# The turned row maxima of the second attention: copied by ScalarE and added by GpSimd instead of added by VectorE

## The reference, cut to what matters

```python
q = (x @ Wq.T).reshape(b, s, H, HD)
k = (x @ Wk.T).reshape(b, s, H, HD)
v = (x @ Wv.T).reshape(b, s, H, HD)
f = jax.nn.log_sigmoid((x @ Wf.T + bf).astype(jnp.float32))
c = jnp.cumsum(f, axis=1)
scores = jnp.einsum('bihd,bjhd->bhij', q, k) * scale
scores = scores + (c[:, :, None, :] - c[:, None, :, :]).transpose(0, 3, 1, 2)
scores = jnp.where(causal[None, None], scores, -jnp.inf)
p = jax.nn.softmax(scores, axis=-1)
o = jnp.einsum('bhij,bjhd->bihd', p, v).reshape(b, s, D)
return o @ Wo.T
```

## Time and profile before

| What | Value |
|---|---|
| Median of three runs | 1497.99 us (1496.64 to 1499.35) |
| The profiled execution | 1496.76 us, its span 1494.9 us |
| Loop of the second attention | from about 838 to 1287 us of the span |
| Its steady unit | 14.04 us (a unit's group 0 starts at 1010.10 and the next one's at 1024.14 us) |
| VectorE, whole span | busy 1147.7 us (77%) |
| TensorE, whole span | busy 1111.0 us (74%) |
| ScalarE, GpSimd, whole span | busy 909.8 us (61%), 469.7 us (31%) |

### The profile page before, as it was taken

How to read it: one execution, slowest core, us unless ns; L and a number is a source line. 1 busy time by engine, 2 the same in 40 slices (tenths; PEclk the granted TensorE clock), 3 DMA queues, 4 the chain that set the end, 5 groups by cost and what they waited for, 6 DMA issues and landing times. The chain is left out here.

```text
span 1494.9 us, 26800 instructions
## 1 busy us (share of the span) xinstructions
PE 1111.0 (74%) x7861; PEld 520.7 (35%) x7861; DVE 1147.7 (77%) x3607; ACT 909.8 (61%) x1823; POOL 469.7 (31%) x676
## 2 busy tenths in 40 slices
PE   1556666666532899994476889999999999677995
PEld 1112222222222566662253432332333333243554
DVE  4699999999979444444856699999999999377664
ACT  1699999999851344332552466666666666356453
POOL 0133233323215677774100122222222222123331
PEclk9755555555555899997697899999999999798998
DMA  2366777777717222224534111111111111400001
GB/s 56 105 121 136 144 144 133 142 139 138 128 41 201 63 77 79 78 78 145 172 107 138 63 57 59 57 57 57 58 58 58 57 57 37 113 1 1 1 14 43
DMA packets 220767, 127.66 MB, mean 85 GB/s; under 512 B 164353, under 2 KB 200321, under 8 KB 220369
## 3 DMA queue, kind: packets, MB, share of 16 engines
q1 hardware_dynamic: 200576, 100.10, 27.4%
q0 software_dynamic: 6320, 15.54, 3.2%
q10 hardware_dynamic: 13728, 10.30, 2.8%
HBM read 54.33 MB, written 37.62 MB: 62 GB/s over the span
## 5 line engine op out<-in xcount | busy, mean ns | idle before, releaser
L1849 ACT ACTIVATE qkv_made<-qkv_lower 128x1024 f32<-128x1024 f32 (+3 forms) x256 | 208.0, 872 | 94.0 <-PE qkv_lower L1666 94.0
L521 PE MATMUL a_sc<-a_k,a_q 16*128 16x512 bf16 (+3 forms) x384 | 165.4, 504 | 123.9 <-DVE a_mx L700 117.3
L2012 DVE CUSTOM_DVE_ANT_0 all_y<-qkv_upper,all_mask 128x384 bf16<-128x384 f32 (+3 forms) x512 | 231.5, 485 | 17.3 <-PE qkv_upper L1630 11.2
L1630 PE MATMUL qkv_upper<-l_k,all_y 64*128 64x512 bf16 (+3 forms) x768 | 208.7, 334 | 48.3 <-DVE qkv_mx L2016 25.6
L1895 POOL TENSOR_SCALAR_AFFINE_SELECT qkv_made<-qkv_made 128x256 f32<-128x256 f32 x256 | 102.5, 406 | 408.7 <-ACT qkv_made L1849 318.7
L700 DVE CUSTOM_DVE_ANT_0 a_rows<-a_sc,all_mask 128x1024 bf16<-128x1024 f32 (+7 forms) x256 | 192.3, 751 | 7.9 <-PE a_sc L521 7.4
L570 ACT ACTIVATE a_rows<-a_rows 128x1024 bf16<-128x1024 bf16 (+7 forms) x256 | 171.3, 669 | 24.3 <-DVE a_rows L710 24.3
L2016 DVE TENSOR_REDUCE qkv_mx<-qkv_upper 128x1 f32<-128x512 f32 x256 | 173.0, 686 | 7.5 <-PE qkv_upper L1630 7.3
L1666 PE MATMUL qkv_lower<-all_y,l_k 64*128 64x384 bf16 (+3 forms) x768 | 173.4, 330 | 7.0 <-DVE all_y L2033 1.2
L1685 PE MATMUL qkv_upper<-qkv_made,qkv_v_heads 128*32 128x384 f32 (+3 forms) x1920 | 177.8, 434 | 0.0
L579 ACT ACTIVATE a_unread<-a_rows 128x1024 bf16<-128x1024 bf16 (+7 forms) x256 | 170.9, 668 | 0.0
(11 more groups left out here) (255 smaller groups left out, 1968.4 us busy)
## 6 DMA issues: line engine op xcount, KB each, us to landing
qkv_made<-out_rows SPq DMA_DIRECT2D x16, 512.0 KB, 8.1
l_k<-k_rows SPq DMA_DIRECT2D x64, 128.0 KB
o_rows<-qkv_made SPq DMA_DIRECT2D x32, 256.0 KB, 2.0
all_y<-q_rows SPq DMA_DIRECT2D x128, 48.0 KB
a_raw<-in_gate ACTq DMA_DIRECT2D x16, 224.0 KB, 3.2
a_raw<-in_up ACTq DMA_DIRECT2D x16, 224.0 KB, 4.1
ride_wd<-in_down SPq DMA_DIRECT2D x1, 3584.0 KB, 17.0
k_rows<-qkv_parts SPq DMA_DIRECT2D x8, 384.0 KB, 3.2
```

The source lines that it names most:

```text
L521: last = nc.tensor.matmul(sc[:, n % 3, lo // 512, 0:w], q_sb[32 * h:32 * h + hd, u % 2, qb * P:(qb + 1) * P], k_sb[32 * h:32 * h + hd, u % ...
L1630: nc.tensor.matmul(row[:, n % SLOTS, 0:w], q_sb[of_head, u % RING, POS[qb] * P:(POS[qb] + 1) * P], k_sb[of_head, u % RING, lo:lo + w], sta ...
L1849: nc.scalar.activation(probs[:, n % GR, lo:hi], st[:, n % 2, lo:hi], ACT.Exp).then_inc(exp_done, 1)
L2012: nc.vector.tensor_tensor_reduce(out=passed[:, n % SLOTS, 0:w], in0=tile[:, 0:w], in1=mask[:, at:at + w], scale=1.0, scalar=-3e38, op0=ALU ...
```

## The change

It takes the addition of the turned maxima off VectorE. ScalarE copies them out of PSUM into a new SBUF tile `beside` (`copy_turned`), in its queue behind the exponent of group 8, and GpSimd adds `beside` to the queries (`add_turned`), in its queue behind `causal` of key block 4. The turning moves from step 8 to step 7, between pieces 2 and 3, and the pieces are spread two to a step. The slot of the turning comes free with ScalarE's copy; the first scores of the next unit wait for GpSimd's addition. `row_free` counts the maxima alone.

```diff
-         (0, 1), (2, 3), (TURN,), (4, 5, 6), (7, 8, 9), (10, 11))
+         (0, 1), (2, TURN, 3), (4, 5), (6, 7), (8, 9), (10, 11))
...
+    maxed_of = {e: i for i, e in enumerate(e for e in entries if e[1] != TURN)}
...
+        beside = c.sb("beside", [P, S], BF16)
...
+            def slot_free(n):
+                if n >= SLOTS:
+                    before = entries[n - SLOTS]
+                    if before[1] == TURN:
+                        pe.wait_ge(turn_copied, before[0] + 1)
+                    else:
+                        pe.wait_ge(row_free, maxed_of[before] + 1)
...
-                        pe.wait_ge(row_free, entry_of[u, TURN] + 1)
+                        pe.wait_ge(turn_added, u + 1)
...
+            def copy_turned(u):
+                act.wait_ge(row_ready, entry_of[u, TURN] + 1)
+                if u:
+                    act.wait_ge(turn_added, u)
+                nc.scalar.copy(beside[:], row[:, entry_of[u, TURN] % SLOTS].bitcast(BF16)).then_inc(turn_copied, 1)
+
+            copy_turned(0)
...
+                    if g == 8 and u + 1 < units:
+                        copy_turned(u + 1)
...
+            def add_turned(u):
+                pool.wait_ge(turn_copied, u + 1)
+                nc.gpsimd.tensor_tensor(out=q_sb[:, u % RING], in0=beside[:], in1=q_sb[:, u % RING], op=ALU.add
+                                        ).then_inc(turn_added, 1)
+
             copy_v(0)
+            add_turned(0)
...
                 for kb in range(TB):
                     causal(u, kb)
+                    if kb == 4 and u + 1 < units:
+                        add_turned(u + 1)
...
-            def add_max(u):
-                n = entry_of[u, TURN]
-                dve.wait_ge(row_ready, n + 1)
-                nc.vector.tensor_tensor(out=q_sb[:, u % RING], in0=row[:, n % SLOTS].bitcast(BF16),
-                                        in1=q_sb[:, u % RING], op=ALU.add).then_inc(row_free, 1)
```

More of the change, by code:

```diff
@@ L1069, in experts @@
         at, pos, cnt = ht[:, 0], dn[:, 0], dn[:, 1]
+        scattered = [c.sem(f"scattered{j}") for j in range(OUT)]
         listing = ("tables", "chain", "ex_ready", "ones_set", "ranked", "marked",
@@ L1078, in experts @@
          made_ready) = (c.sem(n) for n in names)
-        scattered = [c.sem(f"scattered{j}") for j in range(OUT)]
         block = ctx.enter_context(nc.Block())
@@ L1459, in project_and_attend @@
         of_y, of_x = Spread(nc, c, "y"), Spread(nc, c, "x")
[L1460 to L1463, removed]
+        turns = ("row_ready", "row_free", "turn_copied", "turn_added", "m_parts", "m_clear", "st_ready", "exp_done",
+                 "masked", "pv_done", "v_ready", "o_copied", "v_clear")
+        (row_ready, row_free, turn_copied, turn_added, m_parts, m_clear, st_ready, exp_done, masked, pv_done, v_ready,
+         o_copied, v_clear) = (c.sem(n) for n in turns)
         out_stored = [c.sem("out_a"), c.sem("out_b")]
@@ L1626, in row_chunk @@
                     pe.wait_ge(qk_loaded[u % RING], 128 * (u // RING + 1))
-                if n >= SLOTS:
-                    pe.wait_ge(row_free, n - SLOTS + 1)
+                slot_free(n)
                 of_head = slice(64 * h, 64 * (h + 1))
@@ L2007, in max_of @@
                 dve.wait_ge(row_ready, n + 1)
-                if n >= SLOTS:
-                    dve.wait_ge(row_free, n - SLOTS + 1)
+                if n >= SLOTS and entries[n - SLOTS] in maxed_of:
+                    dve.wait_ge(row_free, maxed_of[entries[n - SLOTS]] + 1)
                 if lo + w == (qb + 1) * P:
@@ L2020, in parts_of_max @@
                 m, top = mcol[:, u % 2], mx[:, u % 2, 0]
-                dve.wait_ge(row_free, entry_of[u, NC - 1] + 1)
+                dve.wait_ge(row_free, maxed_of[u, NC - 1] + 1)
                 nc.vector.tensor_tensor(out=top[:, TB // 2:], in0=top[:, TB // 2:], in1=mx[:, u % 2, 1, TB // 2:],
@@ L2028, in parts_of_max @@
                                                in1=m[:, :, :, m_row], op0=ALU.mult, op1=ALU.subtract).then_inc(m_parts, 1)
-            def add_max(u):
-                n = entry_of[u, TURN]
-                dve.wait_ge(row_ready, n + 1)
-                nc.vector.tensor_tensor(out=q_sb[:, u % RING], in0=row[:, n % SLOTS].bitcast(BF16),
-                                        in1=q_sb[:, u % RING], op=ALU.add).then_inc(row_free, 1)
             def maxima(first, end):
                 for u, what in entries[first:end]:
-                    if what == TURN:
-                        add_max(u)
-                    else:
+                    if what != TURN:
                         max_of(u, what)
```

## The result

The changed kernel takes 1527.19 us (median of four, 1524.68 to 1528.36) against 1497.32 us for the kernel before (median of four, 1493.65 to 1499.35). The ratio is 1.02, with a 95% interval of 1.0175 to 1.0225: slower by 30 us, where 26.5 had been worked out (the forecast was 1523 us). The profiled execution took 1524.68 us, its span 1522.9.

What follows compares the result with a forecast made beforehand. No engine is full, so queue order decides; the turning costs VectorE 1.23 us a unit. Units 22.2, last turning 1.9 and opening 2.4 add 26.5 us to 1496.76: 1523 us forecast, eight-in-ten range 1503 to 1553.

Steps and rivals of the forecast that it cites:

- VectorE's 1.23 us a unit: VectorE's wait, add and delay before piece 4 at the turning, removed by the change; not all was expected to count.
- The add: GpSimd's new add of 1024 columns, priced at 2.13 us; bounds 1.00 and 3.47 us.
- The rival of the broadcast row: GpSimd's add costs 3.47 us, the rate of the all-bf16 multiplication with a broadcast operand: 1566 us, chance 8%.
- The copy: ScalarE's new copy of 1024 columns behind group 8, priced at 1.0 us; bounds 0.9 and 1.16 us.
- The lower bound of 1.00 us: Lowest price for GpSimd's add of 1024 columns, taken from the one-input rate.
- The walk: One steady unit followed from step 7 through the engines' queues: 0.74 us longer, 14.78 us instead of 14.04.
- What is late next: After step 10 starts 0.88 us late, group 0, copy out, group 1 and group 3's scores follow; key block 0's values 0.74 late.
- 22.2 + 1.9 + 2.4: Added time: 30 full units at 0.74 us, the last turning 1.9 us, the opening turning 2.4 us; together 26.5 us.
- the opening: The first turning, with scores right behind it: copy and add replace the 0.69 us add, costing 2.4 us.
- the add was faster: Rival: GpSimd adds faster than its two-input rows, at 1.00 us; a unit gains 0.2 to 0.3 us, 1488 us, chance 7%.
- it evened out: Rival: the add takes about 1.4 us or later slack takes the shift back; 1495 to 1501 us, chance 4%.
- that last rival: TensorE's clock drops in one unit in five, these some 5 us longer: 1553 us or more, chance 5%.

Runs made afterwards that it cites:

- Experiment 2: The kernel before with only the new order (turning in step 7, two pieces to a step), VectorE still adding from PSUM: 1496.71 us, ratio 1.0001.
- Experiments 7 and 8: Kernel before with ScalarE's copy out behind group 1, not group 0: alone (7) 1497.92 us; with the new order, VectorE adding (8), 1493.31 us.
- experiment 4: The changed kernel with the add moved from GpSimd to VectorE, from the copy in SBUF, behind its piece 5: 1505.98 us, ratio 1.0065.

## Why the prediction was right

- **What bounds the kernel.** That no single engine did, and that VectorE's 1.23 us a unit would not come back in full, was right. Experiment 2 shows how much could come at all: VectorE's chain set the unit before, but the chain through the first scores is only 0.18 us shorter, and the new order makes it 0.20 longer.
- **The prices.** The add was put at 2.13 us from three two-input rows on a line and measured 2.13. The estimate of 2.25 us, half of the Trainium skill's figure (GPSIMD Engine Reference, section 3.1), is 0.12 too high for this case, and the measurement decides. The rival of the broadcast row (3.47 us) is out, and with it the thought that all-bf16 operands are slower. The copy was put at 1.0 us and measured 1.01. The lower bound of 1.00 us was drawn from a two-input row of 32 columns (245 ns) to a one-input row of 448 (560 ns); from the one-input row of 32 columns (L999, 209 ns) it would be 1.05. Nothing hangs on it.
- **The walk.** By the distance from step 6: transposes 0.96 us predicted and 1.05 measured; start of the add 2.68 and 2.79; first scores 5.76 and 5.89 (4.88 before). The shift in a unit was to be 0.74 and was 0.83. The extra 0.09 is a sum of errors that partly cancel. The transposes start 0.09 late against the walk. `causal` of key block 5 starts 2.07 us after the add and not 2.13, and by the start of its values (5.33 after step 6, 5.30 in the walk) the walk is nearly right again. Those values take 0.56 us and not 0.46, so the first scores are 1.01 us late and not 0.88. Then the slack of that chain against VectorE's takes 0.18 of it and not 0.14. In experiment 2, without the new copy and add, the transposes start 1.05 us after step 6 as well, so their part belongs to the order and not to the new waits. Why they start later behind piece 0 than piece 3 did is not shown.
- **What is late next.** The chain named (first scores, group 0, copy out, group 1, scores of group 3, key block 0) is the one in the trace: the scores of group 3 wait 0.45 us for ScalarE. Experiments 7 and 8 test it with VectorE's add, not in the changed kernel: with the new order, shortening that chain shortens the unit; before the change VectorE's chain to piece 15 set the unit instead.
- **The sum.** 22.2 + 1.9 + 2.4 = 26.5 us predicted; 24.9 (30 x 0.83), 1.9 and 2.9 measured, 29.7. Two terms were undersized: the unit, by 2.7 us in all, and the opening, by 0.5. At the opening TensorE stood for 3.4 us behind the first add, and the granted clock from 834 to 848 us was 0.63 where it had been 0.76 in the same stretch. Whether the opening's extra 0.5 us comes from the clock was not tried.
- **The rivals.** That the add was faster, or that it evened out, didn't come; the clock of the steady unit stayed at 1.00. The price of that last rival, some 5 us a unit at the lower clock, has no row behind it, and no run shows it.

## What to carry to other kernels

Ask of a hole in the busiest engine who would be fed sooner if it closed, before paying for closing it: here it was TensorE at piece 15, and a second chain only 0.18 us shorter would have bound next. The order that closed the hole made that second chain 0.20 us longer, so the unit stayed as it was; the time alone says nothing of this, the two parts of the unit do. When work is handed to another engine, look at what stands behind it in that engine's queue and at what stands behind the instruction that will wait for that: 2.1 us on an engine that idles 10 us a unit cost 0.83, and 0.09 once the waiting matmuls were moved behind the next unit's scores. Where two chains are nearly equally long, a single edit can measure zero, and only the pair shows a gain.

## What the runs showed of the hardware

VectorE's add with both inputs in SBUF and GpSimd's copy, which reads SBUF, hinder each other. Overlapping, the add took 0.94 us and GpSimd's copy 0.77 (means of 23 and 23 in the steady loop); apart, 0.69 and 0.32 or 0.33. The masked maxima, with one input in PSUM and one in SBUF, show nothing of the kind: beside GpSimd's 2.13 us add they kept their 0.69 us. The Trainium skill (SBUF — State Buffer, section "Who interferes with whom") states such a rule: a VectorE instruction with two SBUF inputs contends with a GpSimd instruction that reads SBUF, for a port that they share. The traces agree, as both are longer. They do not show that one waits for the whole of the other: in experiment 4 the last `causal`, the add and the copy all lie between 1012.26 and 1013.38 us, in 1.12 us, and apart they take 0.41, 0.69 and 0.32, together 1.42.

An add of 1024 bf16 columns takes VectorE 0.69 us, whether the first input lies in PSUM or in SBUF, so copying the maxima out first did not make the add cheaper.
